# Another order of one period's steps in the second layer of a two-layer transformer kernel

## The reference

```python
xn = _layernorm(x)
# attention: blocks of rows, 16 heads of 64
latent_kv = xn @ w_kv_down                 # 128 -> 128
k, v = split(latent_kv @ w_kv_up)          # 128 -> 2 x 1024
q = xn @ w_q                               # 128 -> 1024
att = softmax(causal(q @ k.T * scale))
y = (att @ v) @ w_out
# 16 experts, the 8 best of each row, and a shared one
scores = sigmoid(xn @ gate_w.T)
combine = the 8 best of scores + expert_bias, scaled to a sum of 2.826
h = silu(xn @ w_gate[e].T) * (xn @ w_up[e].T)
x = x + y + sum_e combine[e] * (h @ w_down[e].T) + shared expert
```

## Time and profile before

| what | value |
| --- | --- |
| median of 3 runs | 3310.1 us (3309.51 to 3313.13) |
| the profiled execution | 3313.75 us |
| its span, first to last instruction | 3312.0 us |
| mean granted TensorE clock | 0.982 of full speed |
| TensorE busy | 3014.6 us, 91% |
| VectorE busy | 2250.4 us, 68% |
| ScalarE busy | 1767.9 us, 53% |
| GpSimd busy | 1346.1 us, 41% |
| start of the second layer on TensorE | 1276.2 us |
| one `values`, one `down` of four experts on TensorE | 2.3 us, 2.6 us |
| one of the six q or k transfers in SyncE's queue | 0.65 us |
| a row of maxima, from the issue of its transfer to landing | 1.7 us (median) |
| `xnT` of batch 1, of batch 15 | 1365.1 us, 3115.3 us |

### The profile page before, as it was taken

One profiled execution on the slowest core, in us unless ns is written; L12 is line 12 of the kernel. 1 busy time (PEld: TensorE's weight loads), 2 busy tenths in 40 slices (PEclk: granted clock), 3 DMA queues, 4 the chain that ended last, 5 costly groups with the idle time before them and its releaser, 6 DMA issues.

```text
span 3312.0 us, 62003 instructions
## 1 busy us (share of the span) xinstructions
PE 3014.6 (91%) x22724; PEld 1610.2 (49%) x22724; DVE 2250.4 (68%) x4069; ACT 1767.9 (53%) x3674; POOL 1346.1 (41%) x1223
## 2 busy tenths in 40 slices
...
GB/s 114 51 49 49 62 60 59 49 61 49 51 49 49 66 29 131 106 112 119 107 109 104 109 112 110 107 118 113 105 116 106 108 120 104 107 124 103 107 121 71
DMA packets 271901, 297.58 MB, mean 90 GB/s; under 512 B 30832, under 2 KB 235760, under 8 KB 271088
## 3 DMA queue, kind: packets, MB, share of 16 engines
...
...
## 4 chain that ended last, share of the span: by engine, by line
PE 31%; DVE 10%; DMA 9%; SPq 5%; issue 5%; ACT 2%; POOL 1%; DVEq 0%; ACTq 0%; POOLq 0%
DMA l_y_rec<-rec_scratch 7%; PE l_ps_out L1568 5%; SPq L1098 4%; PE l_ps_any L1468 4%; PE l_ps_any L1600 3%; PE l_ps_any L1470 3%; PE l_ps_any L1469 3%; PE l_ps_any L1593 3%; PE l_ps_exp L1551 3%; PE l_ps_exp L1553 2%; DMA l_spread<-route_scratch 2%; PE l_ps_any L1526 2%; DVE l_yT L1409 2%; DVE l_hid L1414 1%; PE l_ps_sum L1579 1%
## 5 line engine op out<-in xcount | busy, mean ns | idle before, releaser
L1185 POOL TENSOR_TENSOR l_hid<-l_hid,l_spread 128x512 f32<-128x512 f32 x256 | 350.3, 1374 | 766.6 <-DVE l_hid L1420 576.8
L614 DVE TENSOR_REDUCE neg_max<-ps_any 128x1 f32<-128x384 f32 (+3 forms) x704 | 417.7, 636 | 268.7 <-PE ps_any L728 264.4
L1272 ACT ACTIVATE l_probs<-l_ps_exp 128x512 f32<-128x512 f32 x640 | 376.4, 596 | 264.6 <-PE l_ps_exp L1555 228.6
L501 ACT ACTIVATE probs<-ps_exp 128x512 f32<-128x512 f32 x640 | 349.1, 602 | 154.4 <-PE ps_exp L743 153.7
L442 POOL TENSOR_SCALAR_AFFINE_SELECT probs<-probs 128x512 f32<-128x512 f32 x256 | 159.4, 635 | 596.7 <-ACT probs L501 596.7
L1391 DVE TENSOR_REDUCE l_neg_max<-l_ps_any 128x2 f32<-128x768 f32 (+2 forms) x384 | 315.3, 862 | 25.4 <-PE l_ps_any L1531 24.8
L1424 DVE TENSOR_TENSOR l_hw<-l_hid,l_hw 128x512 f16<-128x512 f32 x272 | 256.0, 946 | 78.8 <-ACT l_hw L1255 77.5
L1551 PE MATMUL l_ps_exp<-l_q_a,l_k_a 128*128 128x512 f16 (+3 forms) x1024 | 307.1, 302 | 0.3 <-ACT l_probs L1272 0.2
L1568 PE MATMUL l_ps_out<-l_probs,l_v 128*64 128x512 f32 (+3 forms) x2048 | 304.7, 440 | 0.0
L1553 PE MATMUL l_ps_exp<-l_q_b,l_k_b 65*128 65x512 f16 (+3 forms) x1024 | 297.9, 303 | 0.0
L726 PE MATMUL ps_any<-k_st,q_st 120*128 120x128 f16 (+3 forms) x1024 | 252.3, 303 | 39.4 <-DMA k_st<-stack_scratch 38.1
...
## 6 DMA issues: line engine op xcount, KB each, us to landing
l_spread<-route_scratch SPq DMA_DIRECT2D x128, 512.0 KB, 4.6
l_q_a<-l_q_hi SPq DMA_DIRECT2D x256, 128.0 KB, 2.4
l_y_rec<-rec_scratch SPq DMA_DIRECT2D x128, 256.0 KB, 4.4
l_q_b<-l_q_lo SPq DMA_DIRECT2D x128, 128.0 KB, 2.4
l_k_a<-l_k_hi SPq DMA_DIRECT2D x128, 128.0 KB, 2.3
l_k_a<-l_k_lo SPq DMA_DIRECT2D x128, 128.0 KB, 2.4
l_k_b<-l_k_hi SPq DMA_DIRECT2D x128, 128.0 KB, 2.4
...
```

Source lines behind the costliest of these rows:

```text
L501: nc.scalar.activation(probs[:, n % 2, u], ps_exp[:, (10 * g + u) % 3], ACT.Exp, scale=float(HD0 + DR) ** -0.5).then_inc(exp_done.sem, 1)
L614: nc.vector.tensor_reduce(neg_max[:, n % 2, heads[0]:heads[0] + k, t], src, AX.X, ALU.max, negate=True).then_inc(drained["dve"], 1)
L1185: nc.gpsimd.tensor_tensor(at, at, spread[:, c % 3, n % SPREAD], ALU.mult).then_inc(weighted.sem, 1)
L1272: nc.scalar.activation(probs[:, n % 2, u], ps_exp[:, (5 * p + u) % ST_BANKS], ACT.Exp, scale=float(HD1) ** -0.5).then_inc(exp_done.sem, 1)
```

## The change

Only the tuple `ORDER1` changes: the same steps in another order, and with it, the places where SyncE asks for transfers. No instruction is added or taken out on any engine. Where the list is cut between one period and the next also moves, so that some steps bear another number of batches ahead: `("max", 0, 1, 0)` near the head of the old list is `("max", 1, 1, 0)` near the end of the new one. One part of the diff, the piece around the row of transfers for the routing weights:

```diff
 ORDER1 = (
...
-    ("exp", 0, 5, 1), ("rec_in", 0, 0), ("exp", 0, 5, 2), ("max", 0, 3, 3), ("divide", 0, 0), ("up_in", 0, 14),
-    ("gate_in", 0, 15), ("values", 0, 4), ("max", 0, 3, 4), ("qk", 1, 0, 0), ("lat", 1), ("hw", 0, 14),
-    ("exp", 0, 5, 3), ("turn_max", 0, 3), ("up_in", 0, 15), ("divide", 0, 1), ("rec_in", 0, 1), ("cT", 1),
...
+    ("max", 0, 3, 3), ("max", 0, 3, 4), ("sums", 0, 4), ("divide", 0, 0), ("exp", 0, 5, 1), ("gate_in", 0, 15),
+    ("divide", 0, 1), ("exp", 0, 5, 2), ("turn_max", 0, 3), ("hw", 0, 14), ("cT", 1), ("up_in", 0, 15),
+    ("qk", 1, 0, 0), ("rec_in", 0, 1), ("exp", 0, 5, 3), ("qk", 1, 0, 1), ("gate_in", 0, 16), ("hw", 0, 15),
+    ("qk", 1, 0, 2), ("up_in", 0, 16), ("spread_in", 1, 0), ("exp", 0, 5, 4), ("qk", 1, 0, 3), ("exp", 0, 6, 0),
...
 )
```

More of the change, by code:

```diff
@@ L872 @@
[L872 to L876, removed]
@@ new lines @@
+    ("down", 0, 1), ("max", 0, 2, 2), ("exp", 0, 3, 0), ("max", 0, 2, 3), ("exp", 0, 3, 1), ("divide", -1, 7),
+    ("hw", 0, 8), ("exp", 0, 3, 2), ("gate_in", 0, 9), ("up_in", 0, 9), ("norm", 1), ("hw", 0, 9), ("scale", 1),
+    ("exp", 0, 3, 3), ("max", 0, 2, 4), ("res", -1), ("values", 0, 2), ("sums", 0, 1), ("out", -1, 1),
+    ("gate_in", 0, 10), ("spread_in", 0, 6), ("qk", 0, 3, 0), ("exp", 0, 3, 4), ("outT", -1), ("sums", 0, 2),
+    ("up_in", 0, 10), ("turn_max", 0, 2), ("gate_in", 0, 11), ("qk", 0, 3, 1), ("up_in", 0, 11), ("xnT", 1),
```

31 lines of the change are left out of this document (25 added, 6 removed).

## The result

The changed kernel takes **3184.2 us** (median of 3 runs, 3176.99 to 3186.37) where the kernel before takes 3310.1: a ratio of 0.9612, with a 95% interval of 0.9587 to 0.9638. It is faster by 126 us, where the prediction said 96; the range 3160 to 3285 holds it. The profiled execution of the changed kernel took 3176.99 us, the lowest of the three runs, with a span of 3175.3. Lines of the changed kernel are one higher than those of the kernel before.

A forecast was written before the change was run, and what follows sets the result against it. TensorE sets the time, its idle time mostly waits on VectorE. Gains of 1.25, 1.77, 0.9, 1.15, 1.4, 0.8 and 1.3 less 2.2 make 6.4 us per period, 96 us over fifteen: 3214 us, range 3160 to 3285.

The forecast's parts named there:

- first and third division: VectorE's waits for reciprocals there end behind more VectorE instructions; gains of 1.25 and 1.77 us per period.
- routing weights: Read ahead of the k transfers, v copy ahead of `hw`: TensorE's wait on that copy goes, gain 1.15 us per period.
- tails: Matmul ends left uncovered after each TensorE wait: five waits fewer give 0.8 us per period.
- The losses: Costs of the new order at turned maxima, `exp`, routing and other bank fills: 2.2 us per period, upper end 5.5.
- the seventh division: Reads ahead of k transfers; some 3 us of VectorE's wait stays, covered by `values` and `down`; gain 0.9 us per period.
- routing behind two `hw`: VectorE's routing starts later, behind two `hw` on ScalarE: a loss of 0.3 us per period.
- crowded stretch: VectorE before `max` 2, 0 and the `down` behind it: one `hw` leaves, gain 1.4 us per period.
- L1414 row: TensorE's waits in that row, 17.9 us in all, were left as they are, with no gain counted.
- clock: Without the holes at the first and third division, most of 1.7 us per period comes back: gain 1.3.
- The ring gives it back: Rival, 14%: TensorE's four banks lean on VectorE's queue, losses reach 5.5 us per period; 3264 us.
- VectorE and GpSimd in each other's way: Rival, 12%: denser order lengthens VectorE's `hw` and divisions, TensorE loses 3.4 us per period; 3265 us.
- ScalarE held at `scale`: Rival "slower", 9%: next batch's normalisation holds ScalarE for about 7 us, 2 us per period worse if 5 over; 3340 us.

The follow-up runs named there:

- e3: Old order with first and third divisions later, routing weights read and v copied earlier, and seventh division's reads ahead of the k transfers: 3223.5 us.
- e4: e3 with `hw` of expert 6 moved behind `max` 2, 0 and the first `down` behind the first `values`: 3220.1 us.
- e5: e4 with VectorE's routing moved behind `up_in` of expert 13: 3214.1 us.
- a2: Changed kernel with the first read of the routing weights again behind the six k transfers and the v copy behind `hw` 0: 3186.6 us.
- a4: Changed kernel with the reads for the seventh division again behind the six k transfers: 3285.2 us.
- i3: Changed kernel with last maximum of pairs 1 before `qk` 2, 0, `exp` 2, 0 behind `up_in` 7, seventh division behind `max` 2, 1: 3155.7 us.
- i2: Changed kernel with last maximum of pairs 1 before `qk` 2, 0, `exp` 2, 0 behind `up_in` 7, `exp` 2, 3 behind `gate_in` 8: 3167.8 us.

## Why the prediction was right, and where it was not

**Right: what bounds the kernel, and by which mechanism.** TensorE was idle behind VectorE, and VectorE behind transfers. e3 takes away these waits alone and gets 87 of the 126 us. e4 and e5 add some 9; the last 30, up to the changed kernel, are the rearranged fills as a whole, and no run takes them apart. The waits at the first and third division and on the routing weights went: as stalls they were 1.74, 1.91 and 1.52 us, where the prediction had 1.25, 1.77 and 1.15 with part of its 0.8 for tails on top. For the routing weights the two moves that it credits are not what counts in the new order (a2). The losses came mostly at the named places and in the named size: without `max` 2, 2, which belongs to the seventh division, 2.0 against 2.2. Only the 0.3 for the routing behind two `hw` did not show.

**Too small: the crowded stretch.** "I take half of 1.37, all of 0.76" was the cautious half; 1.52 fell to 0.16 and 1.05 went, 2.4 instead of 1.4. e4 shows why one could doubt it, since two moves alone only carry the hole to the next fill. The new order has rearranged the fills around it as well.

**Left out: the L1414 row.** "I leave as they are" was wrong by the whole row, 17.9 us or 1.28 per period, and the waits before `up_in` 12 (0.33 each) went as well. The new order puts the routing behind `gate_in` and `up_in` 13, and `xnT` directly behind fills of the experts; I had read the change of the routing's place only as a loss of 0.3. e5 confirms the routing as the cause of the larger part, and that this move alone gets only part of it.

**Right by luck: the seventh division.** Its gain was taken as 0.9. The 1.33 before `max` 2, 3 are gone and 0.43 are new before `max` 2, 2, which makes 0.9, but both steps under it fell. "A wait of some 3 us stays there": 0.66 stayed in the mean. The reads are asked for 5.7 us earlier than in a4, not 3.9, and in the periods shown land after 5.4 us, not 6.4. And the cover that I relied on for the rest hides little: in a4 5.5 us of waiting beside the same `values` and `down` become 4.2 on TensorE. By that a wait of 3 us would have left some 1.7 on TensorE (an estimate, 3 less the 1.3 that a4 hides), more than the 1.32 of before. In i3, where the division stands behind the maximum, the stall is gone.

**Too large: tails and clock.** 0.8 and 1.3 were to come off TensorE's busy time; 0.76 did. The 1.7 us were not all clock: TensorE is busy for 115.0 us in the mean period before and for 114.1 in one at full clock, so the clock cost 0.9, and the rest of the longer periods was longer waits. All of the 0.9 came back. The tails gave nothing: 114.25 is even 0.15 above 114.1. The five waits' tails are gone, but six places of short stalls are new, of which about 1.0 us hides under recorded ends (v 0.48, of which the waits row shows 0.32; `exp` 2, 3 0.30, of which it shows nothing). The Trainium skill ("TensorE: Matmul & The Clock Gate", Part 1) has the fast clock as something that activity releases and idleness takes back, so that all of it should return with no hole left. The periods' clock of 1.00 agrees with it. It was at 1.00 although holes stayed, of up to 1.7 us.

The terms by size: idle time 8.25 won where 4.3 was predicted, busy time 0.76 where 2.1 was. Two errors of opposite sign, net 2.6 us per period, 37 in fourteen. Between the medians 30 are left: the first layer of the profiled executions gives 6 more, the stretches around the fourteen periods take 2, and the profiled execution lay 3.65 us above the median before and 7.2 below it after. That the whole came out as near as it did is in part luck.

**The rivals.** "The ring gives it back" fell: losses were 2.5, not 5.5, though e4, e5 and i2 show its mechanism at work wherever a single step is moved. "VectorE and GpSimd in each other's way" fell: two groups of VectorE in the whole second layer, to be read against the earlier trace rows:

```profile
L1425 DVE TENSOR_TENSOR l_hw<-l_hid,l_hw 128x512 f16<-128x512 f32 x272 | 258.6, 955 | 59.4 <-ACT l_hw L1256 58.9
...
L1410 DVE TENSOR_TENSOR l_yT<-l_yT,l_y_rec 128x512 f32<-128x512 f32 x128 | 125.6, 982 | 22.1 <-DMA l_y_rec<-rec_scratch 21.9
```

955 and 982 ns, against 946 and 979 over the whole second layer of the kernel before (the 948 and 990 of the earlier trace rows are of fourteen periods): a denser order makes them hardly longer. The rule of the Trainium skill ("SBUF — State Buffer", Summary: rules for kernel authors), that of a VectorE operation with two SBUF inputs and a GpSimd operation that reads SBUF the second waits for the first, may explain why both are above the undisturbed 0.69 us, but that share was paid before as well. "ScalarE held at `scale`" happened in the place named, and cost nothing (ScalarE's timeline):

```profile
2048.51 1.65 ACT L1210 ACTIVATE l_x_in<-l_x_in,l_shift,l_rstd 128x128 f32<-128x128 f32 x4 [0.83 <-DVE l_shift L1368]
2050.06 0.57 ACT L1273 ACTIVATE l_probs<-l_ps_exp 128x512 f32<-128x512 f32 x1
```

The `exp` whose scores TensorE had ready at 2044.4 is taken at 2050.06; TensorE meanwhile runs `values`, `sums` and `out` until 2051.3 and does not wait. VectorE was not the 2 us late that would have decided it.
